# Linear phase: per-head scales spread from four row quadrants of the array, each to its own bank, and the state update placed behind them

## Chip, cores and metric

One core of a Trainium2 chip. The time is that of the device for one launch of the whole kernel, in microseconds; the profile is of one execution. The core has five engines that run their own instruction streams and meet at semaphores: TensorE (PE, with its weight loads shown as PEld), VectorE (DVE), ScalarE (ACT), GpSimd (POOL) and SyncE (SP, which issues the DMAs).

## What is computed

Two sequences of 2048 tokens of 128 features pass four residual blocks: softmax attention with one head, a feed-forward block, a gated linear attention with 16 heads of 64, and the feed-forward block again. The change is in the third. Cut to what matters there:

```python
q = l2norm(silu(x @ Wq)); k = l2norm(silu(x @ Wk)); v = silu(x @ Wv)     # per head of 64
g = sigmoid(x @ Wf - dt_bias); beta = sigmoid(x @ Wb)
def step(state, inp):                       # a scan over the tokens
    o_t = einsum('bhd,bhde->bhe', q_t, state) * g_t
    state = A * state + b_t * (k_t outer v_t)
o = o * rsqrt(mean(o * o, axis=-1) + RMS_EPS) * norm_w     # one scale per token and head
o = (o * sigmoid(x @ Wg + bg)) @ Wo
```

The part that is touched is the last normalization: for each token and head one number, the inverse root of a sum of squares, which has to be multiplied into the 64 features of that head.

## The kernel before, in words

`linear_phase` works in steps m = -2 to 16 over tiles of 128 tokens of both sequences (W = 256 columns). Step m projects tile m+1 (k, v, q), gates and attends tile m, and finishes tile m-1. The recurrence is done in chunks of 64 tokens (c = 0, 1 in each sequence b): `attend` inside a chunk, `recall` from the state, `update` to form the outer products of a chunk into the banks `s_ps[c]`, `fade` (POOL) to decay the old state and `new_state` (DVE) to add both. Every engine runs a list of calls written out by hand in its own `step`; each call waits on semaphores for its data and is never overtaken by a later one.

Most products of PE go through four PSUM banks, handed out in a fixed order by `Ring` (L985 and on): the jobs are "... k2 k3 sq sB v2 b0 b1 b2 b3 v3 q0 q1 q2 q3 y g0 g1 ...", and a job gets the bank of the job four places before it. `free` waits until that earlier job has been read, `taken` and `written` wait for a job's reading and its writing. So b0 follows k3, b1 follows sq, b2 follows sB, b3 follows v2, v3 follows b0, q0 to q2 follow b1 to b3, and q3 follows v3.

The scale of tile m-1 in step m: `sum_squares` (PE, L1585) and `add_totals`, `gather_totals` (DVE) give the sums by token in `scale`; `invert_totals` (POOL, L2156 to L2165) takes the power -0.5 and splits the result into a high part and a low remainder in `parts` (L2163, L2165, 32 elements each for both sequences); `turn_scales` (PE, L1600) transposes `parts` into the job sB; `copy_scales` (ACT, L1982) copies it to `scT`; `spread_scales(m, j)` (PE, L1608), j = 0 to 3, multiplies it by the selector `spread` so that each feature row gets its head's scale, two matmuls of 256 columns into job b*j*. Only 32 of the 128 rows of `parts` are other than zero. `scale_u(m, j)` (DVE, L1781) multiplies bank b*j* into `u`; `high_u` (ACT, L1969) and `low_u` (DVE, L1787) split `u` for `project_out` (PE, L1620 to L1622), which waits for `low_u`. The selectors are made once, by `gpsimd_clear` (L1150 to L1156) and `gpsimd_selectors` (L1164 to L1171), in step -1 on POOL.

What stands in line around it in a middle step:

- PE: `sum_squares` sq, `recall(m,0,1)` (L1554), `update((m,0,1),(m,1,0))` (L1568), `turn_scales`, v2 (three matmuls, L1475 to L1477), four `spread_scales`, v3, q0 to q3 (24 matmuls of 256 columns), `project_out`, and at the end of the step `update((m,1,1),(m+1,0,0))`, which waits for `weigh_v(m+1,0)`.
- DVE: `sum_k(m+1,0)` (L1794), `new_state(m,0,1)` (L1821), `scale_u` x4, `low_u` x4, `sum_k(m+1,1)`, `guard_k` (L1798), `gate_o`.
- ACT: `copy_scales`, silu of v2 (L1939), `square_k` (L2009), `high_u` x4, silu of v3, silu of q0 to q3 (L1947).
- POOL: `invert_totals`, `decay_keys` (L2146), `fade` (L2154), and `coefficients` (L2128), which waits for `guard_k`, then `weigh_v` (L2138).

Step 15 has no next tile, so no v2, v3 or q; after the last step the second feed-forward block (`LastFfn`, `ffn.`) starts, and tile 15 gets its scales between its calls.

Of the kernel before, what the change touches and what calls it, by code (L numbers as in the profile page):

```python
# [15 lines left out]
F32 = mybir.dt.float32  # L16
# [5 lines left out]
P = 128  # L22
# [1031 lines left out]
class LinearTables:  # L1054
# [13 lines left out]
    def make_room(self, nc, sb):  # L1068

        with ExitStack() as whole:  # L1070
            self.w_out = whole.enter_context(nc.sbuf_tensor("lt_w_out", [P, NP, P], F32))
        self.w_out_lo = sb("lt_w_out_lo", [P, NP, P], F32R)
        self.w_out_hi = sb("lt_w_out_hi", [P, NP, P], F32R)
        self.w_beta = sb("lt_w_beta", [P, H])
        self.norm_w = sb("lt_norm_w", [P, 1])
        self.bias_f = sb("lt_bias_f", [P, NP])
        self.bias_g = sb("lt_bias_g", [P, NP])
        self.decay = sb("lt_decay", [P, H, L])
        self.decay_q = sb("lt_decay_q", [P, NP, L])
        self.decay_k = sb("lt_decay_k", [P, H])  # L1080
        self.decay_s = sb("lt_decay_s", [P, NP])
        self.mhalf = sb("lt_mhalf", [P, B * H])
        self.ones = sb("lt_ones", [P, B * H])
        self.zeros = sb("lt_zeros", [P, B, H])
        self.pick = sb("lt_pick", [P, 4, 32])
        self.spread = sb("lt_spread", [P, NP, P], F32R)
        self.parts = sb("lt_parts", [P, B, P], F32R)
        self.state = sb("lt_state", [P, B, NP, D])
# [7 lines left out]

    LOADS = 15

    def sync(self, eng):
# [49 lines left out]
    def gpsimd_clear(self, eng):  # L1149
        eng.memset(self.pick[:, :, :], 0.0).then_inc(self.cleared, 1)  # L1150
        eng.memset(self.parts[:, :, :].bitcast(F32), 0.0).then_inc(self.cleared, 1)
        eng.memset(self.spread[:, :, :].bitcast(F32), 0.0).then_inc(self.cleared, 1)
        eng.memset(self.zeros[:, :, :], 0.0).then_inc(self.cleared, 1)
        eng.memset(self.mhalf[:, :], -0.5).then_inc(self.cleared, 1)
        eng.memset(self.ones[:, :], 1.0).then_inc(self.cleared, 1)
        eng.memset(self.state[:, :, :, :], 0.0).then_inc(self.cleared, 1)  # L1156

    def gpsimd_selectors(self, eng):

        eng.wait_ge(self.cleared, 7)  # L1160
        for r in range(2):
# [4 lines left out]
        eng.wait_ge(self.ones_set, 8)  # L1166
        for odd in range(2):
            parts = [self.const[0:32, C_IDENT + at:C_IDENT + at + H].rearrange("p (i r) -> p i r", r=4)[:, :, 2 * odd:2 * odd + 2]
                     .unsqueeze(3).broadcast_to([32, 4, 2, D]) for at in (0, H)]
            where = self.spread[0:32, 4 * odd:4 * odd + 4, :].rearrange("p i (h e) -> p i h e", h=2)  # L1170
            eng.tensor_tensor(where, parts[0], parts[1], ALU.add).then_inc(self.ones_set, 1)  # L1171
        eng.wait_ge(self.ones_set, 10)

# [142 lines left out]
def linear_phase(nc, X, const, w5_hi, w5_lo, tables, norm, next_norm, weights, out):  # L1316
# [5 lines left out]
    with ctx:  # L1322
# [131 lines left out]
        def _(eng):  # L1454
# [118 lines left out]
            def sum_squares(m, job):  # L1573

                bank = free(eng, m, job)
                if job == "sq":
                    if m == 0:
                        eng.wait_ge(tables.ones_set, 10)
                    eng.wait_ge(s["qsq_ready"], 2 * (m + 1))
                else:  # L1580
                    eng.wait_ge(s["usq_ready"], B * m)
# [20 lines left out]

            def spread_scales(m, j):
                if j == 0:
                    taken(eng, m, "sB")
                bank = free(eng, m, f"b{j}")
                for r in range(2):
                    mm = eng.matmul(ps[bank][:, r * W:(r + 1) * W], spread[:, 2 * j + r, :], scT[:, :], start=True, stop=True)  # L1608
                mm.then_inc(full[bank], 1)

# [21 lines left out]
            def step(m):  # L1632
# [34 lines left out]
                if now:  # L1667
                    sum_squares(m, "sq")
                    recall(m, 0, 1)
                if now and nxt:  # L1670
                    update((m, 0, 1), (m, 1, 0))
                elif now:
                    update((m, 1, 0))
                if prv:
# [3 lines left out]
                if prv:  # L1678
                    for j in range(4):
                        spread_scales(m, j)  # L1680
                if m == LAST:
# [47 lines left out]
            turn_scales(NT)  # L1729
            for j in range(4):  # L1730
                spread_scales(NT, j)
            ffn.keys(eng, 2)
# [19 lines left out]
        def _(eng):  # L1752
# [93 lines left out]
            def step(m):  # L1846
# [16 lines left out]
                if nxt:  # L1863
                    sum_k(m + 1, 0)
                if now and nxt:
                    new_state(m, 0, 1)
                if prv:
                    for j in range(4):
                        scale_u(m, j)
                    for j in range(4):  # L1870
                        low_u(m, j)
# [240 lines left out]
        def _(eng):  # L2112
# [43 lines left out]
            def invert_totals(m):  # L2156
# [4 lines left out]
                eng.wait_ge(s["scale_step"], 3 * m - 2)  # L2161
                high = parts[:, :, 0:H]
                eng.tensor_tensor(high, scale[:, :, :], zeros[:, :, :], ALU.add).then_inc(s["scale_step"], 1)  # L2163
                eng.wait_ge(s["scale_step"], 3 * m - 1)
                eng.tensor_tensor(parts[:, :, H:2 * H], scale[:, :, :], high.bitcast(F32), ALU.subtract).then_inc(s["scale_step"], 1)  # L2165

# [138 lines left out]
```

## Time and profile before

| | |
|---|---|
| median of 3 runs | 860.72 us (859.65 to 861.07) |
| the profiled execution | 856.46 us |
| its span, first to last instruction | 854.5 us |
| TensorE's granted clock, mean | 0.994 of 2.4 GHz |
| busy: PE, ACT, DVE, POOL | 93%, 65%, 64%, 66% |
| linear phase (steps -2 to 15) | from about 252 to about 797 us |

Busy time is the share of the span in which an engine has an instruction in it. Matmuls overlap in the pipeline, so the time that one costs is the distance to the start of the next, not its own duration: a 128x256 matmul is shown with 281 ns and starts 0.12 us after the one before. In a timeline row the numbers are start, length of the merged block, engine, line, and "x8" for eight instructions; brackets hold the idle time of that engine before it and what ended it.

### The profile page before, as it was taken

The page shows a single profiled execution, that of the slowest core. Times are in us where ns is not written, and L with a number is a line of the kernel's source. Part 1 is how long each engine was busy: PE and PEld are TensorE (multiplying, and loading weights), DVE is VectorE, ACT ScalarE, POOL GpSimd, SP SyncE. Part 2 cuts the span into 40 slices and gives each one's busy share as a digit, 9 for nine tenths or more (in the row PEclk, how much of TensorE's full clock was granted, in tenths as well). Part 3 has the DMA queues.
Part 4 walks back from the last instruction along what each step waited for, and adds up shares of the span by engine and source line. Part 5 has one row for each costly group of instructions (what it writes and reads, how often), then busy time and mean ns, then how long its engine had stood idle before and what let it go on. Part 6 is the DMA issues. An engine that isn't in the chain of part 4 may idle for free.

```text
span 854.5 us, 31084 instructions
## 1 busy us (share of the span) xinstructions
PE 798.7 (93%) x13187; PEld 691.1 (81%) x13187; DVE 548.8 (64%) x1267; ACT 557.6 (65%) x1171; POOL 560.7 (66%) x449
## 2 busy tenths in 40 slices
PE   5879999999979999999999999999999999998886
PEld 4658998898867788878888888888888888876676
DVE  4997667674863566566656746665567567567573
ACT  4756555555768677776776776777677767765644
POOL 4971211311538888797797797887977977977522
PEclk9999999999989999999999999999999999999999
DMA  4300000100000000000000000000000000000011
GB/s 139 115 1 20 26 20 8 26 19 13 14 2 1 3 3 3 3 4 2 3 3 3 2 3 3 3 3 3 3 3 3 3 3 2 4 3 3 14 38 49
DMA packets 20423, 12.36 MB, mean 14 GB/s; under 512 B 7872, under 2 KB 19008, under 8 KB 20288
## 3 DMA queue, kind: packets, MB, share of 16 engines
q1 hardware_dynamic: 20288, 10.39, 4.4%
q8 instruction: 105, 1.72, 0.8%
q14 instruction: 30, 0.25, 0.1%
HBM read 8.29 MB, written 2.10 MB: 12 GB/s over the span
## 4 chain that ended last, share of the span: by engine, by line
PE 54%; ACT 6%; POOL 4%; issue 3%; DVE 3%; ACTq 0%; DVEq 0%; POOLq 0%
PE la_ps L1475 9%; PE la_ps L1477 7%; PE la_ps L1476 7%; PE la_o_ps L1538 4%; PE la_o_ps L1554 4%; PE la_s_ps L1568 4%; PE la_ps L1585 3%; PE la_ps L1519 3%; ACT la_u_hi L1969 2%; PE la_ps L1506 2%; PE la_ps L1620 2%; PE la_ps L1621 2%; PE la_ps L1622 2%; ACT n_xn L2009 2%; POOL la_scale L2160 1%
## 5 line engine op out<-in xcount | busy, mean ns | idle before, releaser
L2128 POOL TENSOR_TENSOR la_coef<-la_ssk,lt_mhalf 128x32 f32<-128x32 f32 x16 | 87.0, 5440 | 71.1 <-DVE la_ssk L1798 71.1
L1475 PE MATMUL la_ps<-la_x_hi,w_hi 128*128 128x256 f32 x384 | 116.5, 303 | 2.1 <-ACT la_v L1939 1.0
L1476 PE MATMUL la_ps<-la_x_lo,w_hi 128*128 128x256 f32 x384 | 107.5, 280 | 0.5 <-issue 0.5
L1477 PE MATMUL la_ps<-la_x_hi,w_lo 128*128 128x256 f32 x384 | 107.5, 280 | 0.0
L2160 POOL TENSOR_TENSOR la_scale<-la_scale,lt_mhalf 128x32 f32<-128x32 f32 x16 | 97.4, 6086 | 5.9 <-DVE la_scale L1774 5.7
L1821 DVE TENSOR_TENSOR lt_state<-la_s_ps,la_faded 128x512 f32<-128x512 f32 x62 | 42.6, 687 | 66.1 <-PE la_o_ps L1554 51.9
L1475 PEld LDWEIGHTS la_ps<-la_x_hi,w_hi 128*128 128x128 f32 x384 | 72.1, 188 | 14.5 <-issue 6.2
L530 POOL CAST w_hi<-qkv_w_raw 128x256 fp32r<-128x256 f32 x20 | 7.9, 396 | 109.5 <-PE qkv_xt_ps L573 78.8
L1476 PEld LDWEIGHTS la_ps<-la_x_lo,w_hi 128*128 128x128 f32 x384 | 72.4, 188 | 1.1 <-issue 0.7
L600 PE MATMUL qkv_v_ps<-V,qkv_probsT 128*128 128x128 f32 x544 | 71.8, 278 | 1.0 <-ACT qkv_probsT L706 1.0
L1477 PEld LDWEIGHTS la_ps<-la_x_hi,w_lo 128*128 128x128 f32 x384 | 72.2, 188 | 0.0
L600 PEld LDWEIGHTS qkv_v_ps<-V,qkv_probsT 128*128 128x128 f32 x544 | 67.4, 191 | 5.8 <-ACT qkv_probsT L706 2.8
L1960 ACT ACTIVATE la_gate<-la_ps,lt_bias_g 128x256 f32<-128x256 f32 x128 | 50.0, 482 | 33.5 <-PE la_ps L1477 33.5
L1758 DVE TENSOR_TENSOR la_pT<-la_ps,lt_decay 128x512 f32<-128x512 f32 x64 | 41.1, 683 | 38.4 <-PE la_ps L1519 38.4
L2154 POOL TENSOR_TENSOR la_faded<-lt_state,lt_decay_s 128x512 f32<-128x512 f32 x62 | 64.1, 1044 | 2.2 <-DVE lt_state L1821 2.2
L2146 POOL TENSOR_TENSOR la_k<-la_k,lt_decay_k 128x1024 f32<-128x1024 f32 x32 | 61.0, 1905 | 2.0 <-POOL lt_spread L1171 1.0
L698 ACT ACTIVATE qkv_probs<-qkv_xt_ps,at_ntop 128x512 f32<-128x512 f32 (+3 forms) x48 | 30.4, 633 | 48.0 <-DVE at_ntop L637 47.9
L2138 POOL TENSOR_TENSOR la_v<-la_v,la_coef 128x1024 f32<-128x1024 f32 x32 | 60.2, 1903 | 1.3
L1960 ACT ACTIVATE la_f<-la_ps,lt_bias_f 128x256 f32<-128x256 f32 x128 | 51.5, 472 | 13.7 <-PE la_ps L1477 12.3
L1475 PE MATMUL la_ps<-w_hi,la_x_hi 128*128 128x512 f32 x128 | 56.9, 445 | 0.0
L1939 ACT ACTIVATE la_k<-la_ps 128x512 f32<-128x512 f32 x64 | 38.3, 598 | 26.3 <-PE la_ps L1477 23.3
L1554 PE MATMUL la_o_ps<-la_qdT,lt_state 64*64 64x64 f32 x2048 | 45.8, 222 | 6.6 <-issue 5.5
(225 smaller groups left out, 2423.5 us busy)
## 6 DMA issues: line engine op xcount, KB each, us to landing
qkv_w_raw<-in_w SPq DMA_DIRECT2D x20, 128.0 KB, 2.2
X<-in_x SPq DMA_DIRECT2D x8, 256.0 KB, 3.1
out<-X SPq DMA_DIRECT2D x8, 256.0 KB, 2.3
qkv_cos<-in_cos SPq DMA_DIRECT2D x4, 256.0 KB, 3.0
qkv_sin<-in_sin SPq DMA_DIRECT2D x4, 256.0 KB, 3.9
lt_w_out<-in_w_out SPq DMA_DIRECT2D x4, 128.0 KB, 2.7
qkv_w<-in_w_qkv SPq DMA_DIRECT2D x1, 320.0 KB, 3.6
const<-in_const SPq DMA_DIRECT2D x1, 256.5 KB, 4.2
```

The lines of the kernel that those rows point to most:

```text
L600: mm = eng.matmul(o_ps[n % 2][:, 0:P], probsT[:, (BLK[n] + j) % 2, t * P:(t + 1) * P], V[:, bass.ds(b * NT + kt, 1), :], start=(kt == 0), ...
L1475: eng.matmul(out, l_hi, r_hi, start=True, stop=False)
L1476: eng.matmul(out, l_hi, r_lo, start=False, stop=False)
L1477: return eng.matmul(out, l_lo, r_hi, start=False, stop=True)
L1554: mm = eng.matmul(o_ps[h % 2][rows, part(i, c)], state[own, b, h // 2, :], qdT[own, b, h // 2, chunk(c)], start=False, stop=True, skip_gro ...
L1821: eng.tensor_tensor(state[:, b, :, :], s_ps[c][:, :].rearrange("p (r e) -> p r e", r=NP), faded[:, b, :, :], ALU.add).then_inc(up_read[c], 1)
L1960: act = eng.activation(where[:, c, :], ps[bank][:, r * W:(r + 1) * W], ACT.Tanh, bias=bias[:, c:c + 1], scale=0.5)
L2128: eng.tensor_tensor(coef[:, :], ssk[:, :], mhalf[:, :], ALU.pow).then_inc(s["coef_step"], 1)
L2138: eng.tensor_tensor(own, own, over_d(coef[:, b * H:(b + 1) * H]), ALU.mult).then_inc(s["vb_ready"], 1)
L2146: eng.tensor_tensor(own, own, over_d(decay_k[:, :]), ALU.mult).then_inc(s["kd_ready"], 1)
L2154: eng.tensor_tensor(faded[:, b, :, :], state[:, b, :, :], over_e, ALU.mult).then_inc(s["faded_second" if c else "faded_first"], 1)
L2160: eng.tensor_tensor(scale[:, :, :], scale[:, :, :], powers, ALU.pow).then_inc(s["scale_step"], 1)
```

## The change

The transposed scales are laid out four times, at rows 0, 32, 64 and 96, by writing `parts` with 4 x 32 columns. The selector becomes two blocks of 128 columns in which each quadrant of 32 rows holds its own chunk pair. The spread is one call: it waits for all four banks, and then issues, for r = 0 and 1, one matmul on each row quadrant, each into its own bank. On PE the update comes behind it; on DVE `scale_u` comes ahead of `new_state(m,0,1)`. The clearing of `parts` and `spread` goes.

```diff
-        self.spread = sb("lt_spread", [P, NP, P], F32R)
+        self.spread = sb("lt_spread", [P, 2, P], F32R)
...
-        eng.memset(self.parts[:, :, :].bitcast(F32), 0.0).then_inc(self.cleared, 1)
-        eng.memset(self.spread[:, :, :].bitcast(F32), 0.0).then_inc(self.cleared, 1)
...
-        for odd in range(2):
-            parts = [self.const[0:32, C_IDENT + at:C_IDENT + at + H].rearrange("p (i r) -> p i r", r=4)[:, :, 2 * odd:2 * odd + 2]
-                     .unsqueeze(3).broadcast_to([32, 4, 2, D]) for at in (0, H)]
-            where = self.spread[0:32, 4 * odd:4 * odd + 4, :].rearrange("p i (h e) -> p i h e", h=2)
+        for j in range(4):
+            rows, first, odd = slice(32 * j, 32 * (j + 1)), 2 * (j % 2), j // 2
+            parts = [self.const[rows, C_IDENT + at:C_IDENT + at + H].rearrange("p (i r) -> p i r", r=4)
+                     [:, first:first + 2, 2 * odd:2 * odd + 2].unsqueeze(3).broadcast_to([32, 2, 2, D]) for at in (32 * j, 32 * j + H)]
+            where = self.spread[rows, :, :].rearrange("p i (h e) -> p i h e", h=2)
             eng.tensor_tensor(where, parts[0], parts[1], ALU.add).then_inc(self.ones_set, 1)
...
-            def spread_scales(m, j):
-                if j == 0:
-                    taken(eng, m, "sB")
-                bank = free(eng, m, f"b{j}")
+            def spread_scales(m):
+
+                taken(eng, m, "sB")
+                banks = [free(eng, m, f"b{j}") for j in range(4)]
                 for r in range(2):
-                    mm = eng.matmul(ps[bank][:, r * W:(r + 1) * W], spread[:, 2 * j + r, :], scT[:, :], start=True, stop=True)
-                mm.then_inc(full[bank], 1)
+                    for j, bank in enumerate(banks):
+                        rows = slice(32 * j, 32 * (j + 1))
+                        mm = eng.matmul(ps[bank][:, r * W:(r + 1) * W], spread[rows, r, :], scT[rows, :], start=True, stop=True)
+                        if r == 1:
+                            mm.then_inc(full[bank], 1)
...
-                if now and nxt:
-                    update((m, 0, 1), (m, 1, 0))
-                elif now:
-                    update((m, 1, 0))
                 if prv:
                     turn_scales(m)
                 if nxt:
                     by_token(m, "v2")
                 if prv:
-                    for j in range(4):
-                        spread_scales(m, j)
+                    spread_scales(m)
+                if now and nxt:
+                    update((m, 0, 1), (m, 1, 0))
+                elif now:
+                    update((m, 1, 0))
...
             turn_scales(NT)
-            for j in range(4):
-                spread_scales(NT, j)
+            spread_scales(NT)
...
+                if prv:
+                    for j in range(4):
+                        scale_u(m, j)
                 if now and nxt:
                     new_state(m, 0, 1)
                 if prv:
-                    for j in range(4):
-                        scale_u(m, j)
                     for j in range(4):
                         low_u(m, j)
...
-                high = parts[:, :, 0:H]
-                eng.tensor_tensor(high, scale[:, :, :], zeros[:, :, :], ALU.add).then_inc(s["scale_step"], 1)
+                quads = parts[:, :, :].rearrange("p b (j r) -> p b j r", j=4)
+                high = quads[:, :, :, 0:H]
+                whole, none = (ap[:, :, :].unsqueeze(2).broadcast_to([P, B, 4, H]) for ap in (scale, zeros))
+                eng.tensor_tensor(high, whole, none, ALU.add).then_inc(s["scale_step"], 1)
                 eng.wait_ge(s["scale_step"], 3 * m - 1)
-                eng.tensor_tensor(parts[:, :, H:2 * H], scale[:, :, :], high.bitcast(F32), ALU.subtract).then_inc(s["scale_step"], 1)
+                eng.tensor_tensor(quads[:, :, :, H:2 * H], whole, high.bitcast(F32), ALU.subtract).then_inc(s["scale_step"], 1)
```

## Rows read from the trace of the kernel before

**Rows 1.** The page: busy time of each engine and its share of the span.

```profile
PE 798.7 (93%) x13187; PEld 691.1 (81%) x13187; DVE 548.8 (64%) x1267; ACT 557.6 (65%) x1171; POOL 560.7 (66%) x449
```

**Rows 2.** Timeline of PE in a middle step: start us, length us, line, tiles.

```profile
547.35 0.39 PE L1476 MATMUL la_ps<-w_lo,la_x_hi 128*128 128x512 f32 x1
547.58 0.40 PE L1477 MATMUL la_ps<-w_hi,la_x_lo 128*128 128x512 f32 x1
547.90 1.07 PE L1585 MATMUL la_ps<-la_sq,lt_pick 128*32 128x256 f32 x16
548.90 0.69 PE L1554 MATMUL la_o_ps<-la_qdT,lt_state 64*64 64x64 f32 x32
549.46 1.16 PE L1568 MATMUL la_s_ps<-la_v,la_k 64*64 64x64 f32 x64
550.55 0.44 PE L1600 MATMUL la_ps<-const,lt_parts 128*128 128x128 f32 x2
550.75 0.48 PE L1475 MATMUL la_ps<-w_hi,la_x_hi 128*128 128x512 f32 x1
...
551.52 1.41 PE L1608 MATMUL la_ps<-la_scT,lt_spread 128*128 128x256 f32 x8
552.82 0.50 PE L1475 MATMUL la_ps<-w_hi,la_x_hi 128*128 128x512 f32 x1
...
555.60 0.28 PE L1477 MATMUL la_ps<-la_x_hi,w_lo 128*128 128x256 f32 x1
```

**Rows 3.** Timeline of PE's weight loads, the two of that step that waited for ACT.

```profile
552.43 0.30 PEld L1608 LDWEIGHTS la_ps<-la_scT,lt_spread 128*128 128x128 f32 x2 [0.20 <-ACT la_v L1939]
...
555.94 0.19 PEld L1475 LDWEIGHTS la_ps<-la_x_hi,w_hi 128*128 128x128 f32 x1 [0.26 <-ACT la_v L1939]
```

**Rows 4.** Timeline of ACT in that step.

```profile
551.78 0.60 ACT L1939 ACTIVATE la_v<-la_ps 128x512 f32<-128x512 f32 x1 [0.37 <-PE la_ps L1477]
552.28 1.05 ACT L2009 ACTIVATE n_xn<-la_k 128x1024 f32<-128x1024 f32 x1
553.23 2.18 ACT L1969 ACTIVATE la_u_hi<-la_u 128x512 fp32r<-128x512 f32 x4
555.31 0.58 ACT L1939 ACTIVATE la_v<-la_ps 128x512 f32<-128x512 f32 x1
```

**Rows 5.** Timeline of DVE in that step.

```profile
550.78 0.68 DVE L1821 TENSOR_TENSOR lt_state<-la_s_ps,la_faded 128x512 f32<-128x512 f32 x1
552.07 2.49 DVE L1781 TENSOR_TENSOR la_u<-la_ps,la_u 128x512 f32<-128x512 f32 x4 [0.60 <-PE la_ps L1608]
```

**Rows 6.** Timeline of POOL in that step.

```profile
546.19 0.25 POOL L2165 TENSOR_TENSOR lt_parts<-la_scale,lt_parts 128x32 fp32r<-128x32 f32 x1
...
552.13 1.04 POOL L2154 TENSOR_TENSOR la_faded<-lt_state,lt_decay_s 128x512 f32<-128x512 f32 x1
...
558.38 5.44 POOL L2128 TENSOR_TENSOR la_coef<-la_ssk,lt_mhalf 128x32 f32<-128x32 f32 x1 [5.00 <-DVE la_ssk L1798]
...
564.23 3.77 POOL L2138 TENSOR_TENSOR la_v<-la_v,la_coef 128x1024 f32<-128x1024 f32 x2
```

**Rows 7.** Timeline of PE, the update at that step's end.

```profile
567.06 1.47 PE L1568 MATMUL la_s_ps<-la_v,la_k 64*64 64x64 f32 x64
```

**Rows 8.** Timeline of PE in step 15.

```profile
783.29 0.44 PE L1600 MATMUL la_ps<-const,lt_parts 128*128 128x128 f32 x2 [0.20 <-POOL lt_parts L2165]
...
788.04 0.36 PE L1620 MATMUL la_ps<-la_u_hi,lt_w_out_hi 128*128 128x256 f32 x1 [2.19 <-DVE la_u_lo L1787]
```

**Rows 9.** Timeline of PE at the last call of the spread.

```profile
811.87 1.21 PE L1608 MATMUL la_ps<-la_scT,lt_spread 128*128 128x256 f32 x8 [1.07 <-ACT la_scT L1982]
812.92 0.39 PE L1232 MATMUL la_s_ps<-f_x_hi,fw_wk_hi 128*128 128x512 f32 x1
```

**Rows 10.** Timeline of POOL, the first user behind the selectors.

```profile
263.02 1.91 POOL L2146 TENSOR_TENSOR la_k<-la_k,lt_decay_k 128x1024 f32<-128x1024 f32 x1 [1.01 <-POOL lt_spread L1171]
```

**Rows 11.** Waits of PE's weight loads from 320 to 752 us: total us, times, longest.

```profile
PEld la_o_ps L1554 <- issue: 11.4, 24, 1.2
```

More of the change, by code:

```diff
@@ L1097 @@
     LOADS = 15
+    SELECTORS = 12
     def sync(self, eng):
@@ L1158, in gpsimd_selectors @@
     def gpsimd_selectors(self, eng):
-        eng.wait_ge(self.cleared, 7)
+        eng.wait_ge(self.cleared, 5)
         for r in range(2):
@@ L1166, in gpsimd_selectors @@
         eng.wait_ge(self.ones_set, 8)
-        for odd in range(2):
-            parts = [self.const[0:32, C_IDENT + at:C_IDENT + at + H].rearrange("p (i r) -> p i r", r=4)[:, :, 2 * odd:2 * odd + 2]
-                     .unsqueeze(3).broadcast_to([32, 4, 2, D]) for at in (0, H)]
-            where = self.spread[0:32, 4 * odd:4 * odd + 4, :].rearrange("p i (h e) -> p i h e", h=2)
+        for j in range(4):
[3 more added lines that the diff above has]
+            where = self.spread[rows, :, :].rearrange("p i (h e) -> p i h e", h=2)
             eng.tensor_tensor(where, parts[0], parts[1], ALU.add).then_inc(self.ones_set, 1)
-        eng.wait_ge(self.ones_set, 10)
+        eng.wait_ge(self.ones_set, self.SELECTORS)
     def vector(self, eng):
@@ L1577, in sum_squares @@
                     if m == 0:
-                        eng.wait_ge(tables.ones_set, 10)
+                        eng.wait_ge(tables.ones_set, tables.SELECTORS)
                     eng.wait_ge(s["qsq_ready"], 2 * (m + 1))
```

## Prediction

> **What bounds the kernel now.** I read the page first: TensorE (PE) is busy 93% of the span, no other engine above 66% [rows 1]. So a microsecond counts only where it moves PE. The code that changes runs in the linear phase; the spread is called once in each of steps 1 to 16, eight matmuls a call. The timeline of PE in one middle step is the map for the rest [rows 2]: recall, state update, `turn_scales`, three matmuls of v2, the eight matmuls of the spread, then v3, q0 to q3 and `project_out`, with nearly no idle time. Times below are counted from U = 549.46, the start of the update. v2 starts at U+1.29, the spread at U+2.06, v3 at U+3.36.
>
> Two small stalls stand in that stretch. The last two weight loads of the spread were released by ScalarE (ACT) at 552.43, since bank b3 of the ring is the bank of v2 and v2 must first have left it; and q3 needs the bank of v3: its load was released at 555.94 [rows 3], where the pitch of 0.12 would have put it at 555.72. I take 0.22 us from that. The longest chain that ends there runs through ACT: silu of v2, square of k, four `high_u`, silu of v3 [rows 4].
>
> **The change, part by part, in a middle step.**
>
> *The spread.* Eight matmuls of 256 columns take 1.30 us from U+2.06 to U+3.36 in the middle step [rows 2]. In the last call of all, where no bank is late, they take 812.92 - 811.87 = 1.05 us [rows 9]: some 0.22 for the first and 0.12 for each further one. The trace has no matmul on 32 rows, so the new block must be bounded. Lower end: four at once, thus two rounds of 0.12 and nothing else, 0.24. Upper end: no overlap at all, 1.05, and 0.10 for leaving the mode, 1.15. The nearest row is the sum of squares, which packs four column quarters: sixteen matmuls of 256 columns, four deep, start at 547.90 and the next block at 548.90, so 0.25 a round [rows 2] where its operands are plain fp32. The 64x64 update is near as well: 64 matmuls in 1.09 us [rows 2], 0.017 each, so issuing eight is no limit. Four-way packing is thus seen to work. Plain fp32 costs about 0.20 for 256 columns (two of 128 in `turn_scales`, 550.55 to 550.75 [rows 2]), so four rounds are 0.8 to 0.85 and 0.15 to 0.2 is overhead, the change of mode in it. With fp32r's 0.12: 2 x 0.12 + 0.15 = 0.39, say **0.40**. The Trainium skill (TensorE: Matmul & The Clock Gate, Part 3: Packing small matmuls) measured 3.07 times the speed for four row tiles of 512 columns; as an estimate, 0.94 / 3.07 + 0.15 = 0.46, which would make the final sum 0.8 us smaller. No row here shows it.
>
> *The banks.* The new code waits for all four banks before its first matmul. Before, six matmuls ran while ACT emptied v2; now none does. PE was done issuing v2 at 551.52, and b3 was free for its load at 552.43 [rows 2, 3]: **0.90 us** in which PE stands still, then the block. `copy_scales` is no later than that: it comes before silu of v2 on ACT. b0, b1 and b2 are older banks.
>
> *The update* (1.09 us, 549.46 to 550.55) leaves its place before `turn_scales` and comes behind the spread. This moves `turn_scales` and v2 forward by 1.09 and moves nothing else on PE. It issues no DMA.
>
> *Switches of the array's shape.* Where a 128x128 block is followed by a 128x32 one, the last pitch is 547.90 - 547.58 = 0.32 against 0.23 inside the block [rows 2]: 0.09 a switch. The Trainium skill (TensorEngine Tiling (Array Packing), Key Properties) says that changing the tiling mode drains the engine, which speaks against this change; the trace agrees, with that 0.09. The old order has one switch here (update to `turn_scales`). The new one has four: recall to `turn_scales`, v2 to spread, spread to update, update to v3. The first and the last cost what the old one did and the 1.09 and 0.20 above hold them; v2 to spread lies within the 0.90 of standing still; spread to update is the 0.15 of overhead in my 0.40.
>
> PE therefore: `turn_scales` at U, v2 at U+0.20, v2 issued by U+0.97, standing still to U+1.87, spread to U+2.27, update to U+3.36, v3 at **U+3.36, as before**. The 0.90 saved in the spread is paid back by the 0.90 of waiting for v2.
>
> *What is gained* is the stall before q3. ACT now: silu of v2 is over at U+1.8, square of k by U+2.8, then `high_u`, which follow VectorE (DVE). The spread's second round ends, with 0.28 of matmul time, near U+2.5, so DVE starts `scale_u` at U+2.6, as before (552.07) [rows 5], four in 2.4, to U+5.0. The last `high_u` ends at U+5.65, silu of v3 at U+6.2; its release is near U+6.25. Before it was U+6.48 (555.94). PE, without a stall, is at q3 at 3.36 + 2.90 = U+6.26. So q3 starts some **0.22 earlier**, with no margin. v3 needs the first `scale_u`, ended at U+3.3, and q0 to q2 the others, each with 0.1 to 0.7 to spare.
>
> *DVE.* `new_state(m,0,1)` (0.68, before at 550.78, in idle time) now follows `scale_u` and pushes `low_u`, `sum_k` and `guard_k` back by 0.62 (a quarter of the 2.49 of four such passes is the pitch) [rows 5]. `project_out` follows the six matmuls of q3, so from U+7.0, and takes 6 x 0.12 = 0.7 for each `low_u`; the first of these is there at U+6.3 and the others come every 0.62, so it doesn't wait. GpSimd (POOL) waits 5.00 us for `guard_k` [rows 6], so its `fade` behind `new_state` is covered, but the coefficients start 0.62 late, and `weigh_v` ends at 566.1 + 0.6. The update at the step's end needs it, at 567.06 - 0.22 [rows 7]: the margin of 0.93 shrinks to 0.1. Without the 5.00 us cover each `fade` would cost 1.04.
>
> *`parts`.* Two POOL passes grow from 32 to 128 elements. From 1.88 for 1024 (half of 3.77) and 1.04 for 512 [rows 6] an element is 1.6 to 1.7 ns, so 0.25 becomes 0.41, +0.33 for both (bounds: 0 and 1.0, four times the old price). They ended at 546.4 and are now needed at U = 549.46: hidden. Not so in step 15, where `turn_scales` waits for them [rows 8], and project_out is then held 2.19 us by `low_u`: there +0.33 and 0.1 for the later first bank, **+0.4**; the moved update lies inside that idle time. In the last call (16) `copy_scales`, not `parts`, is what holds the spread (1.07 idle) since ACT is in the feed-forward's work, which I take to cover the 0.33; PE saves 0.6 in the block, and the fourth `low_u` holds it again [rows 9]: 0, bounds -0.6 and +0.4.
>
> *Setup.* Two clears go, and four selector passes of 256 elements replace two of 512, +0.4 by the same slope. The next pass of POOL had waited 1.01 for the selectors [rows 10], which is the most that can be gained; the coefficient pass behind it waits for DVE anyway, so 0.
>
> **The sum.** Fourteen middle steps of -0.22 are -3.1; step 15 is +0.4: **-2.7 us** on the profiled execution's 856.46 (span 854.5), 853.8. The median of the runs shown is 860.72, 4.3 above that execution; I move both by the same: **858.0**. About 0.2% (1.7 us) is what can be told from no change. PE also loses idle time called "issue" in the 64x64 blocks (recall alone 11.4 us of weight loads in 24 places over thirteen steps) [rows 11]. The move shifts where these fall and puts a pause between two dense blocks; I count 0, with 2.5 us either way in the range.
>
> **Rivals.**
>
> *The gain is used up elsewhere.* Either silu of v3 is 0.1 to 0.2 later than worked out, or `weigh_v` is 0.1 to 0.2 late at the update. For it: both margins come out at 0.1 or less. Against: each cannot cost more than the 0.22 gained unless the slip of 0.62 is over 0.93. Result -1.5 to +0.5, so 860.2.
>
> *Slower: the four quadrants do not overlap*, so that the change doesn't do what it says. The place is the spread; its price is 1.15 in place of 0.40, +0.75 a step, less 0.22: 14 x 0.53 = +7.4, with step 15 some +8, **868.7**. It decides from a block of 0.62 upwards. For it: no row has a matmul on 32 rows with fp32r operands. Against: column quarters and 64-row halves do overlap [rows 2].
>
> *Slower: dearer switches.* If entering or leaving row quarters costs 0.25 and not 0.1, both ends of the new block cost 0.30 a step: 14 x 0.08 + 0.4 = +1.5, 862.2; at double that 864.
>
> *The wait for v2 does not hold the block*, if it were free by the time PE comes. Then 0.9 a step goes, -12, 848. Against: silu of v2 can't begin before v2 has ended, and took 0.60 [rows 4].
>
> **How the numbers follow.** Forecast 0.46 (its own range 856 to 859, -4.6 to -1.8), used up elsewhere 0.28, no overlap 0.14, dearer switches 0.08 (of which 0.02 within 0.2%), wait hidden 0.04. Faster by over 0.2%: 0.46 + 0.04 = 0.50. Within: 0.28 + 0.02 = 0.30. Slower: 0.14 + 0.06 = 0.20. The range leaves out the no-overlap and the hidden-wait cases (0.18) and takes in the dearer switches nearly whole: 854.5 (forecast's low end less part of the issue time) to 863.5.
>
> **What would show it.** In the profile after: v2 1.09 earlier against recall; 0.9 us before the spread with silu of v2 as its releaser; a block of 0.4 from the first spread matmul to the update; v3 at U+3.36; no stall at q3; ssk 0.6 later and POOL's wait for it longer; spread-to-spread distances 0.2 shorter. A spread block over 0.6, a stall before q3 or at the update at the step's end for POOL, or no wait for v2, makes the prediction wrong in that step of it.

## The result, and the profile after

The changed kernel takes 874.96 us (median of 4 runs, 871.34 to 877.13) against 860.89 for the kernel before: a ratio of 1.016, 95% interval 1.0131 to 1.019. It is 14 us slower where 2.7 us faster was forecast, and outside the range of 854.5 to 863.5.

First the page of the changed kernel: busy time, and the granted clock in 40 slices.

```profile
PE 792.4 (91%) x13187; PEld 686.0 (79%) x13187; DVE 560.8 (64%) x1267; ACT 564.7 (65%) x1171; POOL 589.9 (68%) x449
...
PEclk9999999999989999999999999999999999998989
```

PE is busy 6 us less than in [rows 1] and the span is 18 us longer (872.5 to 854.5), so the time lost is PE's waiting. POOL is busy 29 us more. Only 7 of that is the two wider passes to `parts`; some 12 are `fade` and the small pass behind it, and 13 the two small passes to `n_rstd` of the input's normalization, all of which take longer for the same work: something holds them.

Next the timeline of PE in a middle step, the counterpart of [rows 2]. The lines are one to five numbers higher: `turn_scales` is L1601, the spread L1611, the update L1569, `project_out` L1624.

```profile
555.38 0.69 PE L1555 MATMUL la_o_ps<-la_qdT,lt_state 64*64 64x64 f32 x32
556.00 0.44 PE L1601 MATMUL la_ps<-const,lt_parts 128*128 128x128 f32 x2
556.20 0.48 PE L1476 MATMUL la_ps<-w_hi,la_x_hi 128*128 128x512 f32 x1
...
557.98 0.51 PE L1611 MATMUL la_ps<-la_scT,lt_spread 32*128 32x256 f32 x8 [0.84 <-ACT la_v L1942]
558.48 1.16 PE L1569 MATMUL la_s_ps<-la_v,la_k 64*64 64x64 f32 x64
...
559.57 0.50 PE L1476 MATMUL la_ps<-w_hi,la_x_hi 128*128 128x512 f32 x1
...
563.16 0.28 PE L1624 MATMUL la_ps<-la_u_hi,lt_w_out_hi 128*128 128x256 f32 x1
...
568.46 0.69 PE L1539 MATMUL la_o_ps<-la_pT,la_v 64*64 64x64 f32 x32
570.21 0.72 PE L1507 MATMUL la_ps<-const,la_k 64*128 64x64 f32 x16 [1.05 <-ACT la_gate L1963]
```

Up to `project_out` PE goes as forecast. With U = 556.00, the end of the recall, v2 starts at U+0.20, the spread at U+1.98 (forecast 1.87), v3 at U+3.57 (3.36), `project_out` at U+7.16 (7.0; before U+7.29). The new loss is in the last row: before the second `turn_k` PE sits idle 1.05 us for ACT's gates, 5 us after the place of the change. From the start of `attend` (568.46) to `turn_k` it now takes 1.75; before it took 0.71:

```profile
562.04 0.69 PE L1538 MATMUL la_o_ps<-la_pT,la_v 64*64 64x64 f32 x32
562.75 0.71 PE L1506 MATMUL la_ps<-const,la_k 64*128 64x64 f32 x16
```

What holds ACT is read on DVE, the counterpart of [rows 5].

```profile
558.56 2.48 DVE L1783 TENSOR_TENSOR la_u<-la_ps,la_u 128x512 f32<-128x512 f32 x4 [1.22 <-PE la_ps L1611]
560.96 0.68 DVE L1823 TENSOR_TENSOR lt_state<-la_s_ps,la_faded 128x512 f32<-128x512 f32 x1
561.56 3.39 DVE L1789 TENSOR_TENSOR la_u_lo<-la_u,la_u_hi 128x512 fp32r<-128x512 f32 x4
564.88 1.21 DVE L1796 TENSOR_REDUCE la_ssk<-n_xn 128x16 f32<-128x1024 f32 x1
...
566.23 1.28 DVE L1809 SCALAR_TENSOR_TENSOR la_u<-la_f,la_o_ps 128x512 f32<-128x512 f32 x2
```

`scale_u` starts at U+2.56, as forecast. But the four `low_u` take 3.39 in place of 2.49. `gate_o` (L1809) ends at U+11.5; before, with U = 549.46, it ended at U+10.1:

```profile
558.23 1.29 DVE L1807 SCALAR_TENSOR_TENSOR la_u<-la_f,la_o_ps 128x512 f32<-128x512 f32 x2
```

On ACT, the counterpart of [rows 4] further on in the step:

```profile
566.23 0.39 ACT L1989 ACTIVATE la_yT<-la_ps 128x256 f32<-128x256 f32 x1 [2.08 <-PE la_ps L1626]
567.54 1.06 ACT L2026 ACTIVATE la_sq<-la_u 128x1024 f32<-128x1024 f32 x1 [0.93 <-DVE la_u L1809]
568.51 2.28 ACT L1963 ACTIVATE la_gate<-la_ps,lt_bias_g 128x256 f32<-128x256 f32 x6
```

`square_u` (L2026) waits 0.93 for `gate_o`. It had not waited before, when it followed `copy_y` at U+10.6:

```profile
559.82 0.38 ACT L1986 ACTIVATE la_yT<-la_ps 128x256 f32<-128x256 f32 x1 [1.99 <-PE la_ps L1622]
560.10 1.05 ACT L2023 ACTIVATE la_sq<-la_u 128x1024 f32<-128x1024 f32 x1
```

The gates g0 and g1 stand behind it, and the transposes of k take their banks. And on POOL, of [rows 6]:

```profile
561.72 1.42 POOL L2157 TENSOR_TENSOR la_faded<-lt_state,lt_decay_s 128x512 f32<-128x512 f32 x1 [1.51 <-DVE lt_state L1823]
563.11 0.70 POOL L2127 TENSOR_TENSOR la_beta<-la_beta,lt_ones 128x32 f32<-128x32 f32 x1
566.38 5.44 POOL L2131 TENSOR_TENSOR la_coef<-la_ssk,lt_mhalf 128x32 f32<-128x32 f32 x1 [2.58 <-DVE la_ssk L1800]
```

The `fade` that `new_state` releases starts 0.16 after the first `low_u`. It takes 1.42 in place of 1.04, the small pass behind it 0.70 where it took 0.25. Both engines are slowed where `fade` and `low_u` meet.

**Where the 18 us of the profiled execution went.** From `turn_scales` of step 1 to that of step 14 it is 449.54 us, 437.95 before: 11.6 more in thirteen steps, 0.9 each. By blocks, as means: the start of the spread after `turn_scales` +1.0, the spread -0.84, v3 to `project_out` -0.34, `attend` to `turn_k` +1.07. From `turn_scales` of step 14 to that of step 16 it is +5.0, and behind that +2.5; both are looked at last. Ahead of step 1 the new kernel is 1.2 ahead. Two profiles of one kernel differ in the loop too: 437.95 and 439.26 for the kernel before (x13), 449.54 and 449.73 for the changed one (x14), 431.87 and 430.25 for the kernel of x8 and x12. A difference of 1.5 us between loops says nothing.

### The profile page after: what moved, and what is told of

The parts are those of the page before. It is cut to its first block and busy times, and to the rows that moved or that the text cites. A ratio compares the mean times of both kernels' runs of the same rounds, so it can differ in the third digit from the quotient of the medians.

```text
span 872.5 us, 31100 instructions
## 1 busy us (share of the span) xinstructions
PE 792.4 (91%) x13187; PEld 686.0 (79%) x13187; DVE 560.8 (64%) x1267; ACT 564.7 (65%) x1171; POOL 589.9 (68%) x449
## 5 line engine op out<-in xcount | busy, mean ns | idle before, releaser
L2163 POOL TENSOR_TENSOR la_scale<-la_scale,lt_mhalf 128x32 f32<-128x32 f32 x16 | 95.5, 5970 | 4.9 <-DVE la_scale L1776 4.9
L2157 POOL TENSOR_TENSOR la_faded<-lt_state,lt_decay_s 128x512 f32<-128x512 f32 x62 | 69.5, 1132 | 22.9 <-DVE lt_state L1823 22.9
L1963 ACT ACTIVATE la_f<-la_ps,lt_bias_f 128x256 f32<-128x256 f32 x128 | 51.5, 472 | 13.0 <-PE la_ps L1478 11.7
L1783 DVE TENSOR_TENSOR la_u<-la_ps,la_u 128x512 f32<-128x512 f32 x64 | 39.7, 682 | 24.1 <-PE la_ps L1611 24.1
```

Source lines behind the costliest of these rows:

```text
L1963: act = eng.activation(where[:, c, :], ps[bank][:, r * W:(r + 1) * W], ACT.Tanh, bias=bias[:, c:c + 1], scale=0.5)
L2157: eng.tensor_tensor(faded[:, b, :, :], state[:, b, :, :], over_e, ALU.mult).then_inc(s["faded_second" if c else "faded_first"], 1)
L2163: eng.tensor_tensor(scale[:, :, :], scale[:, :, :], powers, ALU.pow).then_inc(s["scale_step"], 1)
```

## The experiments

Theory L: DVE is late. `new_state` ahead of `low_u` costs 0.62, and the `fade` that it releases meets `low_u` for 0.85 more; that goes by `gate_o`, `square_u` and the gates to PE. Theory J, later: the joint wait for the four banks starts `scale_u` 1.0 late and so uses up the slack. Rivals: PE itself (idle time and switches of shape), or the order alone. All ratios are to the kernel before on the same chip, "loop" is the time from `turn_scales` of step 1 to that of step 14 in the profile (437.95 before).

### x1: DVE's order alone, in the kernel before

```diff
-                if now and nxt:
-                    new_state(m, 0, 1)
                 if prv:
                     for j in range(4):
                         scale_u(m, j)
+                if now and nxt:
+                    new_state(m, 0, 1)
+                if prv:
                     for j in range(4):
                         low_u(m, j)
```

> The kernel before with one edit: on DVE new_state(m,0,1) stands behind the four scale_u, as in the changed kernel; PE, POOL and the spread are untouched. Theory L (late DVE: new_state ahead of low_u costs 0.62, and the fade that it releases on POOL runs beside low_u, where one low_u takes 1.53 instead of 0.68; gate_o, square_u and the gates follow, and PE's second turn_k waits for their banks): about 1.1 to 1.3 us a step lost before turn_k, so 874 to 878, with low_u up to 1.5 us. Rival P (it is PE: the standing still before the spread and the switches of the array's shape): unchanged, 861.

884.74 us, 1.0287 (1.0259 to 1.0315), loop 458.07. Rival P falls: PE's own program is untouched, and it is slower than the changed kernel. `low_u`, all of the run (ns, min/median/max):

```profile
L1787 DVE TENSOR_TENSOR la_u_lo<-la_u,la_u_hi x64: 677/681/1535, 322.9 to 843.8; 128x512 fp32r<-128x512 f32 x64
```

The longest was 689 in the kernel before. The loss is larger than the expected 14 to 17 us since a second wait appeared, ahead of the update (0.42 a step in the loop), which x9 isolates; `attend` to `turn_k` takes 0.94 a step more.

### x2: the late fade

```diff
-                    fade(m + 1, 0, 0)
                     coefficients(m + 1)
...
                 if now and nxt:
                     fade(m, 1, 1)
+                if nxt:
+                    fade(m + 1, 0, 0)
```

> The changed kernel with one edit: on POOL fade(m+1,0,0) stands behind fade(m,1,1) instead of ahead of the coefficients, so nothing of POOL runs beside low_u. Theory L: low_u back to 0.68 each, ssk 0.85 earlier, the wait of the second turn_k down from 1.07 to about 0.2 a step, so 875 - 14 x 0.85 = 863. Rival P: 875 as it is. If the 0.62 of new_state alone were the cause and not the meeting with fade: 871 or more.

870.3 us, 1.0113 (1.0088 to 1.0139), loop 444.50. PE's waits from 335 to 735 us (total us, times, longest):

```profile
PE la_ps L1611 <- ACT la_v L1942: 10.1, 12, 0.8
...
PE la_ps L1601 <- POOL lt_parts L2170: 3.2, 7, 0.8
PE la_ps L1507 <- ACT la_gate L1963: 2.6, 11, 0.3
```

The wait before `turn_k` falls from 12.0 us in the same window to 2.6, as L says, and the longest `low_u` is 793 ns. Less than 12 us is gained since POOL now comes late with `parts` (L2170): the late `fade` pushes the inverse roots. That wait was not expected, and the time alone lies where the reading "the 0.62 alone" (871 or more) had put it; it is the trace that speaks for L. This is not the place to cure the meeting.

### x3: the quadrants without the new order

```diff
+                if now and nxt:
+                    update((m, 0, 1), (m, 1, 0))
...
                 if prv:
                     spread_scales(m)
-                if now and nxt:
-                    update((m, 0, 1), (m, 1, 0))
```

with `new_state` ahead of `scale_u` again.

> The changed kernel with the order undone: the update back ahead of turn_scales on PE, new_state back ahead of scale_u on DVE; the four quadrants, their banks' joint wait and the wider parts stay. Theory L: the block is 0.44 but starts 1.0 later, so DVE and ACT start scale_u and high_u about 1.0 later, and PE waits at q3 or at turn_k for it: +0.8 to +1.0 a step, 872 to 875. Rival P: two switches less than the changed kernel and the same wait, 870 to 872, with the idle time before the spread only.

882.5 us, 1.0249 (1.022 to 1.0277), loop 456.92. The timeline of PE in a middle step:

```profile
563.32 0.51 PE L1611 MATMUL la_ps<-la_scT,lt_spread 32*128 32x256 f32 x8 [0.84 <-ACT la_v L1941]
564.64 0.50 PE L1476 MATMUL la_ps<-w_hi,la_x_hi 128*128 128x512 f32 x1 [0.82 <-DVE la_u L1783]
```

Both theories gave less (875 at most), and neither named the place: `attend` to `turn_k` is 0.71, as before, and no `low_u` is stretched. After the 0.84 for v2, v3 waits 0.82 more, because all of `scale_u` starts only when the block ends and v3 needs the bank of the first. With the update behind the spread this second wait is covered. So the new order repairs a part of what the joint wait breaks. This profile has three stretches of 3.4 us at half the clock inside the loop, which the others don't have; they can be up to 5 of its 19 us over the kernel before.

### x4: the new order without the quadrants

```diff
                 if prv:
                     for j in range(4):
                         spread_scales(m, j)
+                if now and nxt:
+                    update((m, 0, 1), (m, 1, 0))
```

(taken away ahead of `turn_scales`), and DVE's order as in x1.

> The kernel before with the order alone changed (update behind the spread on PE, scale_u ahead of new_state on DVE); the spread stays on 128 rows with its bank by bank waits. Theory L: no wait at q3 (-0.22), scale_u 1.1 earlier, but low_u meets fade (+0.85), so DVE ends within -0.5 to +0.4 of before: 857 to 865. Rival P: one switch more, 862.

859.64 us, 0.9992 (0.9972 to 1.0012), loop 437.81: no difference. Here too the longest `low_u` is 1533 ns, but `scale_u` starts 1.0 earlier and that pays for it. So the quadrants with their joint wait cost 15 us on the new order and 22 on the old one (x3), and the order by itself nothing. What the loss consists of, x5 to x7 take apart.

### x5: bank by bank

```diff
-                banks = [free(eng, m, f"b{j}") for j in range(4)]
-                for r in range(2):
-                    for j, bank in enumerate(banks):
-                        rows = slice(32 * j, 32 * (j + 1))
+                for j in which:
+                    bank = free(eng, m, f"b{j}")
+                    rows = slice(32 * j, 32 * (j + 1))
+                    for r in range(2):
                         mm = eng.matmul(ps[bank][:, r * W:(r + 1) * W], spread[rows, r, :], scT[rows, :], start=True, stop=True)
```

> The changed kernel with the loops of the spread turned round: for each quadrant its own bank's wait, then its two matmuls, so that only b3 waits for v2. Everything else as changed. Theory J (the joint wait starts scale_u 1.0 late, and with new_state and the meeting with fade that is more than the 0.6 of slack of the chain gate_o, square_u, gates, second turn_k): PE saves 0.3 in the block and the 1.07 before turn_k, so 875 - 14 x 1.3 = 857. Rival O (the order on DVE alone is the cause, the wait of no account): only the 0.3, 871.

865.62 us, 1.0086 (1.0057 to 1.0115), loop 440.30: between the 857 of theory J and the 871 of rival O. 9 us of the 14 go with the joint wait. The remainder is theory L's: `low_u` still meets `fade`, and `attend` to `turn_k` takes 0.58 a step more than before. I had expected that wait to vanish. In seven of the thirteen steps it is 0.25 to 0.32, since PE, without the wait at q3, comes earlier and so finds ACT later. In the other six it is 0.83 to 1.02, since there the first `low_u` meets a second pass of POOL, `decay_keys`, and the four take up to 4.11. Step 4, on DVE and on POOL:

```profile
419.84 4.02 DVE L1789 TENSOR_TENSOR la_u_lo<-la_u,la_u_hi 128x512 fp32r<-128x512 f32 x4
...
418.68 1.91 POOL L2149 TENSOR_TENSOR la_k<-la_k,lt_decay_k 128x1024 f32<-128x1024 f32 x1
420.55 1.50 POOL L2157 TENSOR_TENSOR la_faded<-lt_state,lt_decay_s 128x512 f32<-128x512 f32 x1
```

### x6: the update between b2 and b3

```diff
                 if prv:
-                    spread_scales(m)
+                    spread_scales(m, (0, 1, 2))
                 if now and nxt:
                     update((m, 0, 1), (m, 1, 0))
...
+                if prv:
+                    spread_scales(m, (3,))
```

> As x5, and on PE the state update stands between b2 and b3, so that it covers silu of v2. Theory J: no standing still before the spread, two more switches of the array's shape, 0.6 to 0.7 less from v2 to v3 than in the changed kernel; DVE is then the late one through low_u beside fade, and part of the gain comes back before turn_k: 855 to 859. Rival O: 865.

864.85 us, 1.0061 (1.0032 to 1.009), loop 439.89. v2 is fully covered, yet the time is that of x5: what PE gains it waits for before `turn_k` (`attend` to `turn_k` 1.48 in place of 1.29). An engine that is late elsewhere takes the gain: the expectation was 6 to 10 us too low, and the time is the one that rival O gave (865). What speaks against O is x5, where the waits alone brought 9 us, and x10 below.

### x7: new_state behind low_u

```diff
                     for j in range(4):
                         scale_u(m, j)
-                if now and nxt:
-                    new_state(m, 0, 1)
-                if prv:
                     for j in range(4):
                         low_u(m, j)
+                if now and nxt:
+                    new_state(m, 0, 1)
```

> The changed kernel with new_state(m,0,1) behind the four low_u on DVE: fade then runs beside sum_k and not beside low_u. Theory L (low_u is stretched by the fade beside it): low_u 0.68 each, the wait before turn_k from 1.07 to about 0.2, and unlike with the late fade no wait for parts: 863. If sum_k is stretched as low_u was: 875.

862.3 us, 1.0044 (1.0024 to 1.0065), loop 439.18. Two adjacent calls exchanged in the changed kernel bring back 10 to 12 us of the 14 (10.4 in the loop, 11.7 by the medians, each against its own kernel before). `fade` now runs beside `sum_k`, and neither is stretched (`fade` at most 1.05, `sum_k` at most 1.22), on DVE and on POOL:

```profile
587.84 2.49 DVE L1789 TENSOR_TENSOR la_u_lo<-la_u,la_u_hi 128x512 fp32r<-128x512 f32 x4
590.25 0.69 DVE L1823 TENSOR_TENSOR lt_state<-la_s_ps,la_faded 128x512 f32<-128x512 f32 x1
590.85 1.21 DVE L1796 TENSOR_REDUCE la_ssk<-n_xn 128x16 f32<-128x1024 f32 x1
...
591.01 1.04 POOL L2156 TENSOR_TENSOR la_faded<-lt_state,lt_decay_s 128x512 f32<-128x512 f32 x1 [3.87 <-DVE lt_state L1823]
```

This is the most direct proof of the meeting: `gate_o` still stands behind `new_state`, so the 0.62 is still in its way, and yet it ends at U+10.6 in place of U+11.5. `attend` to `turn_k` is 1.04 a step and not 0.71, since in five of the thirteen steps `decay_keys` reaches into the first `low_u` (0.91 to 1.15 in place of 0.68). The shares of x5 and x7 overlap: taken together (x10) they give 15.5 us of the loop, alone 9.2 and 10.4.

### x8 and x12: x6 and x7 together

> x6 and x7 together: update between b2 and b3, new_state behind low_u. Theories J and L: nothing stands in the way of what PE saves, 0.6 to 0.7 from v2 to v3 and the 1.07: 848 to 853, less than the kernel before. If another engine takes over: 857 or more.

854.85 us, 0.995 (0.9929 to 0.9971), loop 431.87: faster than the kernel before, and 2 us above the expected 848 to 853. A second run of the same kernel:

> x8 once more beside x11 on the same chip: 855, 0.4 to 0.7% below the kernel before.

855.42 us, 0.9971 (0.9954 to 0.9987), loop 430.25: 0.3% less than the kernel before where 0.4 to 0.7% was expected; the sign is the same. The wait before `turn_k` is gone but for two steps of x8 and one of x12, in which `decay_keys` stretches the first `low_u` (to 1.75 in x8), and the timeline of PE in x8 shows no idle time from v2 to v3:

```profile
579.21 0.51 PE L1612 MATMUL la_ps<-la_scT,lt_spread 32*128 32x256 f32 x6
579.65 1.16 PE L1569 MATMUL la_s_ps<-la_v,la_k 64*64 64x64 f32 x64
580.74 0.50 PE L1612 MATMUL la_ps<-la_scT,lt_spread 32*128 32x256 f32 x2
581.17 0.50 PE L1476 MATMUL la_ps<-w_hi,la_x_hi 128*128 128x512 f32 x1
```

### x9: DVE's order alone, but behind low_u

x1 with `new_state` behind `low_u`.

> The kernel before with one edit: on DVE new_state(m,0,1) stands behind the four low_u (in x1 it stood ahead of them). Theory L: the slip of 0.62 alone, without the fade beside low_u, which is about what the chain to turn_k can bear: 861 to 866 against 885 in x1. Rival (any place of new_state behind the spread costs, since POOL's fade and the update wait for it): 875 or more.

872.16 us, 1.0159 (1.0133 to 1.0184), loop 448.03: outside what either theory gave, and nearer the rival's 875. The wait before `turn_k` is as good as gone (`attend` to `turn_k` 0.77), so the slip of 0.62 alone is what that chain can bear, as L said. But PE has a new one, in its waits from 335 to 735 us:

```profile
PE la_s_ps L1568 <- POOL la_k L2146: 5.0, 4, 1.5
```

The update, early on PE in this kernel, waits for `decay_keys` of POOL, since POOL is late. The coefficients start 0.7 later; and in about half of the steps the two small `n_rstd` passes take 1.2 and 1.6 where they took 0.2 and 0.7, beside `gate_u`'s passes of DVE (L1813), which have both inputs in SBUF too. The second of them in x9, and in the kernel before:

```profile
579.82 1.56 POOL L107 TENSOR_TENSOR n_rstd<-n_rstd,n_mhalf 128x2 f32<-128x2 f32 x1
...
572.28 0.69 POOL L107 TENSOR_TENSOR n_rstd<-n_rstd,n_mhalf 128x2 f32<-128x2 f32 x1
```

In the changed kernel the update comes 2.4 us later and doesn't notice. From recall to the end of that wait it is 0.58 a step, 7.5 of the 10.1 us that x9's loop is longer. So the loop of x1 less that of x9, 10 us, is the meeting of `low_u` and `fade`, and of x9's own 14 about half is this wait; 3.6 more lie behind step 14, with the clock (below).

### x10: x5 with new_state behind low_u

> x5 (bank by bank waits) with new_state behind low_u, so it differs from x7 in the joint wait alone. Theory J: the joint wait costs PE 0.2 in the block and starts scale_u 0.9 later; 0.2 to 0.4 a step less than x7's 862: 856 to 859. Rival: the joint wait costs nothing once nothing meets low_u: 862.

857.17 us, 0.9985 (0.9966 to 1.0004), loop 434.06. As expected by J (856 to 859). Against x7 the bank by bank waits gain some 5 us: theory J holds without the meeting too.

### x11: x8 on 128 rows

```diff
                 if prv:
-                    for j in range(4):
+                    for j in range(3):
                         spread_scales(m, j)
+                if now and nxt:
+                    update((m, 0, 1), (m, 1, 0))
+                elif now:
+                    update((m, 1, 0))
+                if prv:
+                    spread_scales(m, 3)
```

in the kernel before, with the update taken away ahead of `turn_scales` and `new_state` behind `low_u`.

> x8 without the quadrants: the spread on 128 rows as before, update between b2 and b3, new_state behind low_u. Six matmuls of the spread take 0.7 where the six on quadrants take 0.5, and two take 0.3 to 0.35 where they take 0.43, with one switch less at each end. If the quadrants bring little in themselves: 854 to 858, as x8 or 1 to 3 more. If they carry x8's gain: 860.

853.05 us, 0.9936 (0.9913 to 0.996), loop 430.84: the fastest of all by its median, 1 us below what was expected, and at least level with x12 on the same chip (855.42; loop 430.25). Its PE timeline:

```profile
579.51 0.91 PE L1608 MATMUL la_ps<-la_scT,lt_spread 128*128 128x256 f32 x6
580.35 1.16 PE L1568 MATMUL la_s_ps<-la_v,la_k 64*64 64x64 f32 x64
581.45 0.51 PE L1608 MATMUL la_ps<-la_scT,lt_spread 128*128 128x256 f32 x2
581.79 0.40 PE L1475 MATMUL la_ps<-w_hi,la_x_hi 128*128 128x512 f32 x1
```

From the start of the spread to v3 it is 2.28 us; on quadrants, in x8, 1.96, of which the pitch of v2's last matmul before it and of v3's after it take back 0.2. The quadrants are worth 0.1 us a step of PE at most, which this measurement cannot tell from nothing. The gain of x8 over the kernel before is the order's, on PE and DVE together. What the update between b2 and b3 alone brings is x12 against x10 on one chip: 1.8 us by the medians, 3.8 in the loop.

### x13 to x15: the end of the linear phase

In the profile of the changed kernel the two steps from `turn_scales` of step 14 to that of step 16 took 5.0 us more, with 6.8 us at half the clock (1.2 GHz) in them. Is that the change's?

> The kernel before, profiled a second time. If the half-clock stretch at step 15 or 16 comes by chance: it is there, and the two steps take 60 us or more in place of 57.5. If it belongs to the change: none, 57.5 again.

> The changed kernel, profiled a second time: steps 1 to 14 take 449 to 450 us again, the wait before the second turn_k is 1.07 a step; by the chance theory the stretch at half clock may be missing, by the other it is there.

> The changed kernel with the update ahead of turn_scales in step 15 alone. If the stretch follows from PE's idle time in that step: no or a later half-clock stretch, 872. If chance: 875 with it.

Each row is that stretch: from and to, length, busy times (and instructions) of PE, PEld, DVE, ACT and POOL, the granted clock, then the DMAs. The kernel before, its second profile (x13), the changed kernel, its second profile (x14), and x15:

```profile
752.86:810.36 57.50, 49.79 (x923) 43.05 (x919) 38.45 (x83) 33.46 (x66) 37.56 (x26) 1.00 0.02 4
```

```profile
756.64:814.16 57.52, 49.51 (x925) 42.84 (x919) 38.36 (x83) 33.49 (x66) 37.58 (x26) 1.00 0.02 4
```

```profile
763.28:825.80 62.52, 52.19 (x988) 44.97 (x982) 40.37 (x84) 34.31 (x67) 41.31 (x28) 0.95 0.02 6
```

```profile
762.85:825.89 63.04, 51.72 (x988) 44.77 (x983) 40.59 (x84) 34.28 (x67) 41.36 (x28) 0.95 0.02 6
```

```profile
762.62:828.14 65.52, 54.10 (x988) 47.26 (x982) 40.48 (x84) 34.27 (x67) 41.91 (x28) 0.90 0.02 5
```

x13 is 860.3 us (1.0003, 0.998 to 1.0025), x14 874.91 (1.0162, 1.011 to 1.0214), x15 875.26 (1.016, 1.0116 to 1.0204). Twice without a drop before, twice with one in the changed kernel: it is not chance. x15 has it as well, and more of it (13.7 us at half), so the place of the update in step 15 is not its cause. Every kernel of x1 to x12 has a drop in these two steps too (6.8 to 17.1 us at half), the faster ones included. In the changed kernel it comes at 798.3 us of the one profile and at 778.0 of the other, behind idle times of PE of 1.53 and 1.15 us; but in the same stretch the kernel before stands still for 2.19 [rows 8] and keeps its clock. What sets it off stays open. The +2.5 behind step 16 goes with the clock as well: 0.97 there in the profile of before, 0.92 in x13, 0.90 in both of the changed kernel. The drop is not worth all of the 5 us in the medians either: of the 14.1 us, the loop's 11.6 leave 2.5 for everything else.

## Why the prediction was wrong, point by point

**The part on PE was right.** The block on quadrants takes 0.44 in most steps (0.40 forecast), the standing still before it cost 1.0 (0.90), the wait at q3 is gone (-0.34 from v3 to `project_out`; -0.22 forecast), and `project_out` comes 0.18 a step earlier (0.22 forecast). The rivals of no overlap, of dearer switches and of the hidden wait did not happen. Of the switches of shape the one from recall to `turn_scales` can be read by itself: 0.06 (0.63 for the recall, 0.57 where the update followed it).

**The step that failed is "DVE"**: a wait left out, and a cost put at nothing. It named the work that is pushed back by `new_state` ("`low_u`, `sum_k` and `guard_k` back by 0.62") and followed it to POOL, but not to `gate_o`, which stands behind `guard_k` in the same list, and from there to `square_u`, the gates and the banks of `turn_k`. That chain had 0.6 us to spare: `gate_o` ended at U+10.1 and `square_u` started at U+10.6 (x9 bears this out: a slip of 0.62 leaves 0.77 in place of 0.71). In the changed kernel `gate_o` slipped by 1.45 (0.62, and 0.85 of the term below), and PE came 0.18 earlier: 1.45 - 0.58 + 0.18 = 1.05, and 1.07 was measured. The margin that was watched, `weigh_v` against the update at the step's end, did hold, but by luck: the coefficients slipped by 1.46, more than its 0.93, and there were 0.37 us left only because PE had lost 1.07 before `turn_k`.

**In the same step a term is missing**: `low_u` beside `fade`. The text said that `fade` is covered by POOL's 5.00 us of waiting. It is, for POOL; but it then runs beside four passes of DVE with both inputs in SBUF, and these grow from 2.49 to 3.39. x2 and x7 take the meeting away, each in another way, and with it 0.85 and 0.74 us a step of the wait; x9 against x1 prices it at 10 us in the loop. The Trainium skill (SBUF — State Buffer, 🔬 SBUF: two separate sides) says that a GpSimd op that reads SBUF and a VectorE op with two SBUF inputs lock each other out, each for a whole instruction. The traces agree: one `low_u` of the four takes 1.53, 0.85 more, while `fade` (1.04 alone) holds, and `sum_k` (at most 1.22) and `scale_u` (at most 0.69), with one input in SBUF, are not stretched in any run. That rule stood against this change and should have been a rival.

**`parts`**: 0.47 a pass in place of 0.41, hidden in the middle steps, as said. **Step 15**: +0.4 forecast; it can't be read since the clock falls there. **POOL and the coefficients**: late by 1.46 rather than 0.62, and without effect only for the reason just given. **The clock**: no term of the sum; some or all of the 2.5 us of the medians that the loop doesn't hold may be its, and its cause is open.

**The joint wait** was priced rightly for PE and wrongly left out as a term for the others. "`scale_u` starts at U+2.6, as before" is right, but only since the update had made room of 1.0 us: without the joint wait it would have started at about U+1.6, as in x4 and x5, and the slip of DVE would have been paid. x5 gives it 9 us, x10 against x7, where nothing meets `low_u` but now and then `decay_keys`, some 5.

## To carry to other kernels

Where a call is moved in one engine's list, follow everything behind it in that list to its reader, to the end of the step, not only the chain whose margin looks smallest; a busy engine with small slacks everywhere waits at the one not looked at. Ask what a moved instruction releases, and what that will run beside: on DVE and POOL a pass of one can be lengthened by the other, and a shift of 0.6 us anywhere can bring two such passes together that had missed each other (x5, x9). Before packing matmuls tighter, see whether the packing needs all of its banks at once; here the better order, with the late bank covered by other work, was worth 3 to 5 us (x8, x12, x11), on 128 rows too (x11), the packing itself nothing that could be measured.

## What the runs showed of the hardware

- Eight matmuls of 32 rows and 256 fp32r columns on four row quadrants start and give way to the next block in 0.44 us in most steps (0.50 in the one shown) where eight on 128 rows take 1.05 without a wait [rows 9], each from the first of them to the first matmul of the next block.
- A DVE pass of 128x512 with two SBUF inputs beside a POOL pass of the same size: 1.53 in place of 0.68, and POOL's 1.42 in place of 1.04; a POOL pass of 0.25 took 0.70. Beside a POOL pass of 128x1024 (1.91) one such DVE pass took 1.75 (x8). A DVE reduction of 128x1024 beside the pass of 1.04 kept its 1.21 (x7).
- In the two steps before `turn_scales` of step 16 the granted clock fell to 0.95 of full speed on average (6.8 us at half, 1.2 GHz) in both profiles of the changed kernel and in neither of the kernel before. It fell there in all thirteen other profiles as well (0.87 to 0.94), even where only the order on DVE was changed (x1, x9).
